# A Flamingo block with attention and mixture of experts on one core: filler products on TensorE in six known waits, wider router products, two steps placed later

## The reference

```python
x = x + jnp.tanh(g_xattn[0]) * _L0_xattn_ref(_layernorm(x, axis=-1), ctx_1024, ...)
x = x + jnp.tanh(g_ffn[0]) * _L0_ffn_ref(_layernorm(x, axis=-1), router_w, ...)
```

```python
logits = x2 @ router_w                      # (2048, 8)
probs = jax.nn.softmax(logits, axis=-1)
top_p, top_e = jax.lax.top_k(probs, K)      # K = 2
...
h = h + jnp.where(m, jax.nn.gelu(xd @ w_in[e] + b_in[e]), 0.0)
y = y + jnp.where(m, h @ w_out[e] + b_out[e], 0.0)
...
out = jnp.zeros((T, Dm), x.dtype).at[st].add(y * sp[:, None])
```

## Time and profile before

| | |
|---|---|
| profiled execution, whole time | 297.43 us |
| its span | 295.5 us |
| runs: median (lowest, highest) | 298.29 (298.21, 299.31) us |
| PE busy | 256.1 us, 87% of the span |
| PE weight loads | 226.7 us, 77% |
| DVE / ACT / POOL busy | 158.0 / 127.8 / 151.5 us |
| mean clock granted to PE | 0.931 of full speed |

### The profile page before, as it was taken

One profiled execution on the slowest core, in us unless ns is written; L12 is line 12 of the kernel. 1 busy time (PEld: TensorE's weight loads), 2 busy tenths in 40 slices (PEclk: granted clock), 3 DMA queues, 4 the chain that ended last, 5 costly groups with the idle time before them and its releaser, 6 DMA issues.

```text
span 295.5 us, 5845 instructions
## 1 busy us (share of the span) xinstructions
PE 256.1 (87%) x1806; PEld 226.7 (77%) x1806; DVE 158.0 (53%) x501; ACT 127.8 (43%) x304; POOL 151.5 (51%) x184
## 2 busy tenths in 40 slices
PE   8889889989998999789949759979999999999920
PEld 4676557867886989768738749869999999999920
DVE  3884857436563435656503382923683634347765
ACT  5344512624243670032250442456556565666630
POOL 8757968185588210006781027076347775445540
PEclk9977979999999997799987998989999999999985
DMA  7900068639323000001325002534235337299455
GB/s 225 348 21 1 0 211 286 204 85 326 106 87 93 2 0 1 2 0 71 108 72 155 23 20 97 167 115 152 84 115 171 111 111 249 53 352 340 138 188 196
DMA packets 25838, 37.60 MB, mean 127 GB/s; under 512 B 3497, under 2 KB 22954, under 8 KB 25714
## 3 DMA queue, kind: packets, MB, share of 16 engines
q1 hardware_dynamic: 21074, 20.15, 22.6%
q0 software_dynamic: 3744, 10.24, 9.5%
q10 hardware_dynamic: 992, 6.84, 6.7%
HBM read 24.88 MB, written 18.39 MB: 146 GB/s over the span
## 4 chain that ended last, share of the span: by engine, by line
PE 48%; DVE 18%; POOL 13%; issue 12%; ACT 4%; DMA 3%; ACTq 0%; POOLq 0%; DVEq 0%
PE pV L1289 17%; POOL y_rows L574 8%; PE pM L1289 7%; PE pG L1289 7%; PE pS L1391 6%; POOL slots L566 4%; PE pM L1353 4%; DVE mx L889 3%; DVE st L843 2%; PE pS L1614 1%; PE pS L1642 1%; PE pG L1323 1%; DMA yc<-y_rows 1%; PE pM L1449 1%; DMA x_sb<-in_x 1%
## 5 line engine op out<-in xcount | busy, mean ns | idle before, releaser
L574 POOL DMA_INDIRECT y_rows<-y_sb,dst_i x46 | 45.9, 997 | 33.9 <-ACT y_sb L792 28.5
L1289 PE MATMUL pV<-vb,prob 123*128 123x136 f32 (+1 forms) x320 | 46.4, 300 | 2.4 <-DVE c_sb L903 1.6
L1289 PEld LDWEIGHTS pV<-vb,prob 123*128 123x128 f32 (+1 forms) x320 | 43.7, 208 | 5.0 <-issue 3.4
L1219 DVE TENSOR_TENSOR hT_lo<-pS,hT_hi 128x256 fp32r<-128x256 f32 x46 | 19.5, 424 | 48.2 <-ACT hT_hi L786 47.9
L648 ACT ACTIVATE prob<-pS 123x512 f32<-123x512 f32 (+1 forms) x40 | 22.3, 594 | 29.3 <-PE pS L1391 29.0
L889 DVE TENSOR_REDUCE mx<-pM 128x4 f32<-128x308 f32 x56 | 24.1, 472 | 17.5 <-PE pM L1353 16.6
L566 POOL DMA_INDIRECT slots<-z2a,pos_u x16 | 15.8, 989 | 30.2 <-DVE pos_u L1123 25.8
L779 ACT ACTIVATE h_sb<-pM 128x256 f32<-128x256 f32 x46 | 17.6, 383 | 27.9 <-PE pM L1289 26.6
L566 POOL DMA_INDIRECT slots<-z2b,pos_u x16 | 15.4, 961 | 23.3 <-DVE pos_u L1123 18.5
L1353 PE MATMUL pM<-kb_hi,qT_hi 128*128 128x308 f32 x64 | 21.1, 393 | 7.0 <-DVE mx L889 3.4
L1289 PE MATMUL pM<-win_hi,xT_hi 128*128 x92 | 26.5, 288 | 0.0
(11 more groups left out here) (216 smaller groups left out, 653.2 us busy)
## 6 DMA issues: line engine op xcount, KB each, us to landing
xg<-slots SPq DMA_DIRECT2D x46, 128.5 KB, 3.1
slots<-in_empty ACTq DMA_DIRECT2D x1, 3983.5 KB, 15.6
yc<-y_rows SPq DMA_DIRECT2D x10, 256.0 KB, 5.2
x_sb<-in_x SPq DMA_DIRECT2D x4, 512.0 KB, 7.7
stage<-in_w_in SPq DMA_DIRECT2D x8, 256.0 KB, 2.7
stage<-in_w_out SPq DMA_DIRECT2D x8, 256.0 KB, 2.7
slots<-in_empty ACTq DMA_DIRECT2D x1, 1927.5 KB, 7.7
out<-x_sb SPq DMA_DIRECT2D x6, 256.0 KB, 2.2
```

Of the source, the lines that this page charges most:

```text
L574: pool.indirect_dma_start(out=y_rows[int(j >= JB)], out_offset=bass.IndirectOffsetOnAxis(ap=dst_i[:, j:j + 1], axis=0), in_=y_sb[:, j % YR ...
L1219: nc.vector.tensor_tensor(hT_lo[:, j % 2, :], pS[:, 1, 0:D], hT_hi[:, j % 2, :].bitcast(F32), ALU.subtract).then_inc(h_lo, 1)
L1289: last = nc.tensor.matmul(out, l, r, start=(n == 0), stop=(n == len(pairs) - 1))
```

## The change

Four things are done.

1. A helper `keep_busy(out, w, n)` makes `n` products of 128 by 128 by 512 whose result nobody reads. It is called at six places of PE's list: 5 products in the first `head_scores` loop, 3 and 4 about the first `head_scores(1, 0, ...)`, 6 behind `ranks(0)`, 4 ahead of the second hidden tile's transpose (`j` = 2 in the loop), 6 ahead of `project(3)`.
2. The router's product takes its 8 columns twelve times over, so that it writes 96 columns for each token tile; `take_logits` copies only the first 8 of each.
3. Block 2: on PE `transpose_z2(2)` and `logits(2)` stand later among the `weigh(3, 1, i)`; on ACT all of block 3's `exp` stand ahead of `norm2(2)`; on POOL `inv_std(1, 2)` stands after 8 of stage 0's 16 sends and not after 11.
4. Block 3: `norm2`, `z2T`, `logits`, `take`, `choose_0`, `choose_1`, `ranks`, `count`, `place`, `experts` each stand one step `j` later.

```diff
+REP = 12
 AFTER = {
     "count_1": 0, "place_1": 1, "experts_1": 3, "split": 1, "project": 2, "residual": 3, "stats": 5,
-    "norm2": 6, "z2T": 10, "logits": 11, "take": 11, "choose_0": 12, "choose_1": 13,
-    "ranks": 14, "count": 14, "place": 15, "experts": 16, "gates": 22,
+    "norm2": 7, "z2T": 11, "logits": 12, "take": 12, "choose_0": 13, "choose_1": 14,
+    "ranks": 15, "count": 15, "place": 16, "experts": 17, "gates": 22,
 }
...
                 for t in range(SIZE[s]):
                     send(s, 0, t)
+                if s == 0:
+                    inv_std(1, 2, var2, rstd2)
...
-                        if s == 0 and t == 2:
-                            inv_std(1, 2, var2, rstd2)
...
-            exp(3, 5)
-            exp(3, 6)
+            for s in range(5, 2 * CH):
+                exp(3, s)
             norm2(2)
-            exp(3, 7)
-            exp(3, 8)
             copy_z2(2)
-            exp(3, 9)
...
+                got = pL[b][:, 0, 0:BLK * REP * E].rearrange("p (t c) -> p t c", c=REP * E)
+                nc.vector.tensor_copy(lg[:, b * BLK:(b + 1) * BLK, :], got[:, :, 0:E]).then_inc(lg_ready, 1)
...
+            def keep_busy(out, w, n):
+                for _ in range(n):
+                    nc.tensor.matmul(out, w[:, 0:P], w[:, 0:BN], start=True, stop=True)
...
+                    last = product(pL[b][:, 0, i * REP * E:(i + 1) * REP * E].rearrange("p (r e) -> p r e", e=E),
+                                   [(z2T[:, k, i * P:(i + 1) * P],
+                                     rw[:, k, :].unsqueeze(1).broadcast_to([P, REP, E])) for k in range(2)])
...
+                if i == 0:
+                    keep_busy(pS[:, 0, :], wq_flat, 5)
...
                     transpose_max(0)
+                    keep_busy(pV[:, 1, :], wq_flat, 3)
                     head_scores(b + 1, 0, 0)
+                    keep_busy(pV[:, 1, :], wq_flat, 4)
...
             ranks(0)
+            pe.wait_ge(exp_done, 2 * CH * 3)
+            pe.wait_ge(stage_used, 1)
+            keep_busy(pS[:, 0, :], w_hi[0], 6)
...
-            transpose_z2(2)
             scores(3, 1, 2)
             weigh(3, 1, 0)
+            weigh(3, 1, 1)
+            transpose_z2(2)
+            weigh(3, 1, 2)
             logits(2)
-            for i in range(1, BLK):
-                weigh(3, 1, i)
+            weigh(3, 1, 3)
...
                 pe.wait_ge(h_ready, j + 1)
+                if j == 1:
+                    keep_busy(pM[:, 1, :], w_hi[0], 4)
...
                 if j == AFTER["project"]:
+                    keep_busy(pM[:, 1, :], w_hi[0], 6)
                     project(3)
```

More of the change, by code:

```diff
@@ L949, in take_logits @@
                 dve.wait_ge(lg_ps, b + 1)
-                nc.vector.tensor_copy(lg[:, b * BLK:(b + 1) * BLK, :].rearrange("p t e -> p (t e)"),
-                                      pL[b][:, 0, 0:BLK * E]).then_inc(lg_ready, 1)
+                got = pL[b][:, 0, 0:BLK * REP * E].rearrange("p (t c) -> p t c", c=REP * E)
+                nc.vector.tensor_copy(lg[:, b * BLK:(b + 1) * BLK, :], got[:, :, 0:E]).then_inc(lg_ready, 1)
             nc.vector.memset(zT_hi[:, 0, :].bitcast(F32), 0.0).then_inc(warm_ready, 1)
@@ L1311, in _ @@
                                              for k in range(2)]).then_inc(k_ps, 1)
+            def keep_busy(out, w, n):
+                for _ in range(n):
+                    nc.tensor.matmul(out, w[:, 0:P], w[:, 0:BN], start=True, stop=True)
+            wq_flat = wq_hi[:].rearrange("p k n -> p (k n)")
             def transpose_z(b):
@@ L1457, in logits @@
                 for i in range(BLK):
-                    last = product(pL[b][:, 0, i * E:(i + 1) * E],
-                                   [(z2T[:, k, i * P:(i + 1) * P], rw[:, k, :]) for k in range(2)])
+                    last = product(pL[b][:, 0, i * REP * E:(i + 1) * REP * E].rearrange("p (r e) -> p r e", e=E),
+                                   [(z2T[:, k, i * P:(i + 1) * P],
+                                     rw[:, k, :].unsqueeze(1).broadcast_to([P, REP, E])) for k in range(2)])
                 last.then_inc(lg_ps, 1)
```

## The result

| | kernel before | changed kernel |
|---|---|---|
| runs: median (lowest, highest), 4 each | 298.25 (295.31, 299.31) us | 289.23 (288.44, 290.10) us |
| profiled execution, whole time | 297.43 us | 288.44 us |
| its span | 295.5 us | 286.6 us |
| mean clock granted to PE | 0.931 | 0.967 |

Ratio 0.971, interval 0.964 to 0.979: the change makes the kernel 2.9% faster. 286.8 was predicted, with 283.5 to 292.8.

A forecast was written before the change was run, and what follows sets the result against it. PE's list was taken as the bound: its work, its waits and its clock. 297.43 - 2.2 - 1.2 - 1.6 - 4.4 - 0 - 2.6 + 0.3 + 0.2 = 285.9 us profiled, so 286.8 predicted, range 283.5 to 292.8.

The forecast's parts named there:

- first rival: The clock does not answer to the fillers: 292.9 us, or 290 with half the clock terms; chance 0.29, half or whole.
- fillers' price, four router sets' width: Cost charged for the fillers' drains and short overhangs, 0.3 us, and for the wider router products, 0.2 us.
- place 1: 19.1 to 25.9 us, PE at half clock over value products and transposes: 2.2 us gained, bounds 0 and 2.8.
- place 2: 39.6 to 42.9 us, mostly wide score products at half clock: 1.2 us gained, bounds 0 and 1.65.
- place 3: 114 to 125 us, `weigh`, head scores and transposes of maxima at half clock: 1.6 us gained, bounds 0 and 1.65.
- block 2: Norm and logits, 145 to 166 us: 4.74 us wait exchanged for one at tile 0; 4.4 us gained, bounds 3.4 and 4.9.
- `project(3)`: Projection at 176.03 us gets 1.7 us shorter, but PE then waits at tile 8: gain 0, bounds 0 and 1.7.
- the three places: The half-clock stretches at 19.1 to 25.9, 39.6 to 42.9 and 114 to 125 us: 5.0 us gained together.
- block 3: Norm one step later: 1.87 us wait removed, half-clock stretch from 196.7 us partly gone; 2.6 us gained, bounds 1.4 and 3.3.
- new wait: PE idle for tile 0, 156.4 to 160.7 us, 4.3 us; low clock behind it charged at 0.1 us.

The follow-up runs named there:

- e9: The changed kernel unedited, run again on another chip: 290.30 us, ratio 0.988 to the kernel before.
- e1: Changed kernel with all six sets of fillers out, router width and moved steps kept: 290.44 us, ratio 0.978.
- e2: Changed kernel without any fillers and with the router's product back to 8 columns, only the moves left: 291.60 us, ratio 0.985.
- e3: Changed kernel without the ten fillers in the expert loop (second hidden tile, ahead of the last projection): 288.96 us, ratio 0.976.
- e4: Changed kernel with block 3's norm and all that follows it one step earlier again, as before the change: 290.51 us, ratio 0.983.
- e7: Changed kernel with `transpose_c(3)` ahead of the wait for tile 0, no fillers added: 318.75 us, ratio 1.017.
- e6: Changed kernel with 15 more fillers in the wait for tile 0: 316.59 us, ratio 1.007.
- e8: Changed kernel with `transpose_c(3)` ahead of the wait for tile 0 and 13 fillers ahead of it: 316.40 us, ratio 1.012.
- e11: Changed kernel with 15 more fillers in the wait for tile 0 and 9 in that for tile 8: 288.15 us, ratio 0.980.
- e12: Changed kernel with e8's edit, 9 fillers at tile 8, and POOL's `inv_std` of block 2's first norm one weight split earlier: 288.71 us, ratio 0.983.
- e10: Changed kernel with block 2's parts back as before on POOL, ACT and PE (the kernel of e5): 291.22 us, ratio 0.989.
- e5: Changed kernel with block 2's parts back as before on POOL, ACT and PE: 313.52 us, ratio 1.001.

## Why the prediction was right, and where its sizes were not

The first result, 289.23, lies in the range and in the interval of the forecast (284.5 to 289.5), but by 0.3 us only, and 2.4 above the number; it is nearer to the 290 that the first rival gave if it was half true. That it fell on the right side is in part luck: on e9's chip the same kernel took 290.3. Its terms against the two profiles:

| step | predicted | measured (term) |
|---|---|---|
| fillers' price, four router sets' width | +0.5 | inside the terms below |
| place 1 | -2.2 | -2.4 |
| place 2 | -1.2 | -1.4, of which 1.2 lost again by 62 us |
| place 3 | -1.6 | -1.65 |
| block 2 | -4.4 | -4.5 at `transpose_c(3)`, -3.1 at stage 1's sends |
| `project(3)` | 0 | 0 (+0.5 at tile 8) |
| block 3 | -2.6 | -2.6 |
| last awaited load of results | 0 | +0.7 (4.61 us to landing, 3.94 before) |
| ahead of place 1, and outside the span | 0 | -0.2 |
| sum | -11.5 | -9.0 |

**The mechanism** held: fillers in a wait keep the clock up behind it. Place 3 shows it by count: the clock falls there in three of three profiles without fillers, behind a wait of 1.62 us, and in none of eleven with them; if the fillers did nothing, the three falls would meet just these three of the fourteen profiles once in 364 times. At the projection it falls, at 170 to 176 us, in all four profiles without fillers (before, e1, e2, e3), and in none of the six with them on the chips where nothing else stops PE. At tile 0 it falls in all five profiles with block 2 moved whose wait there is unfilled (changed kernel, e3, e4, e7, e9) and in none of the four with fillers (e6, e8, e11, e12). e11 also shows what two such waits are worth by themselves (2.1 us by the medians). Place 2 is half a case: the falls at 38.7 to 40.7 us are gone in all eleven, but six have one at 48 us in their stead. At place 1 the falls at 19 and 20 us of before and e2 are gone, but e1, without fillers, has none there either, because its early fall delayed PE until the wait was gone. So the first rival (the clock does not answer) falls as a mechanism. Its price is another matter, see the three places below.

The rule of the Trainium skill, "TensorE: Matmul & The Clock Gate", section "HAM oscillation", puts the fall down to longer idle gaps. That fits the falls at the waits of 4.74 and 4.02 us (the prediction overlooked the first of these when it said that no such gap stands ahead of the falls), but not those behind 1.40, 1.62 and 1.87 us; there the measurement decides.

**Place 2** was right for its stretch and wrong for what follows. DVE's step ahead of POOL's `inv_std` (line 846) took 0.83 us where it had taken 0.17, beside a POOL instruction, with whose end it ends (45.17 and 45.14 us), and PE waited 0.66 us longer for the maximum at 45.60. Another 0.43 went at 51.81, where PE waited 0.37 us for ACT's `m_sb`, which stands behind the norm of block 2, and that waits for POOL's `nb`: POOL's weight splits had not moved with place 2, and `nb` came only the 2.5 us sooner that place 1 had given, while PE was 3.9 ahead. The prediction's sentence "all that follows, POOL's sends too, moves forward by them" was wrong by these 1.2 us. Both causes are read from one pair of profiles; no run has shown either alone (e12 moved POOL's step, but its partner e9 lacks the wait).

**Block 2** is the term that failed. The new wait was predicted well (4.3 us, measured 4.02; `transpose_c(3)` near 156, measured 156.82). What failed is "less 0.1 in this light stretch": the fall of clock at the new wait lasts 6.7 us and costs stage 1's sends 1.4 us. e11 confirms the size, 1.2 of it won back by fillers. And against e10 the whole move, 4.4 in the sum, is worth 0.9 us in the medians, with ranges that overlap, though 3.1 in the spans of the two profiles; it removes a wait and opens one behind which both profiles of the changed kernel show a fall. With no fillers (e2) the two moves give 5.4, so the terms may not be independent: if 1.3 to 1.6 of it is block 3's as in e4, about 4 is block 2's there.

**`project(3)`** was right to be 0, by its own reason: tile 8 waited 2.57 us (2.3 predicted), and e3, without the ten fillers, lost nothing. Behind this wait the clock fell again (182.2 to 185.5 us), as the prediction had feared under block 3.

**Block 3** measured -2.6 in the pair of profiles, but e4 finds 1.3 to 1.6, about the lower bound of 1.4: in e4's profile the wait that comes back is 0.68 us and not 1.87, and the clock holds behind it, so the clock's part of the term is missing.

**The three places** are the same case. 5.0 predicted, 5.4 in the pair of profiles, 1.5 in e3 against e1 by medians, where the ranges overlap, so that in time the fillers' part is not clear of the spread. The profile of before had the clock low at all three places. That of e1 had it low at two; its third fall stands ahead of place 1 (11.5 to 18.2 us) and is one that kernels with fillers have too, yet it makes 1.8 of the 5.0 us between the profiles of e1 and e3. Other executions of these kernels can hardly have all three falls: e1's fastest has a mean clock of 0.967 and takes 288.89 us. The kernel before ran from 290.8 (clock 0.968) to 300.4 us (0.914) on e9's chip, the changed one from 289.2 to 290.6. So what the change buys is in large part that the long executions go: 9.6 us of spread (13 runs) became 1.4 (4 runs). For the fillers alone e1 (288.9 to 295.3, 6 runs) and e3 (288.1 to 290.0, 4 runs) point the same way, with too few runs to settle it. By the fastest executions the change is worth 1.6 us on that chip, by the medians 5.1, and on the first one 9.0.

Still open: what stops the engines on e5's chip, whether the change gains anything there, why DVE's first norm comes later in some executions, why the clock falls at about 14 and 48 us in some and not in others behind like waits, and what the first 18 fillers are worth in time.

## What to carry to other kernels

Where the granted clock falls behind a short wait of TensorE, independent products in that wait hold it up, and they cost nothing here as long as the wait outlasted them; look next for the wait that the gain opens, since the clock can fall behind that one too. When a step is moved so that one wait is exchanged for another, price the new wait with the slow stretch behind it, from a row of the same kind, and do not charge it at nothing. And read more than one profile of a kernel whose clock falls: a term read from a single execution is the term of that execution, not of the median.

## What the hardware showed that I had not expected

- In two of eleven executions of one list (e6, e9) the clock fell over products of 512 columns that kept PE full (3.40 of 3.40 us busy at 0.50 in e9's window), behind waits of 0.52 and 0.62 us; e7 and e10 have waits of 0.52 and 0.6 us there and kept the full clock.
- The clock fell 2.5 us into a wait of 4.02 us and stayed at half for 6.7 us, of which PE worked 5.05; at the end of a wait of 2.57 us it fell for 3.3 us, all of them worked. Filled with products that left 0.27 and 0.65 us of idling, such waits are followed by none (e11).
- 16 router products of 96 columns take 2.02 us, against 1.91 for 8 columns: twelvefold width for 0.1 us.
- The same kernel took 313.5 us on one chip and 291.2 on another, with equal times up to 136 us.
